# Two-layer vision tower with a graph-gated expert stage: how the edge keys reach their bins is changed

## The chip, the cores and the metric

The kernel runs on one core of a Trainium2 chip, as one program with one launch. Its time is the device time in microseconds (us); the engines are TensorE (PE, with its weight loads as PEld), VectorE (DVE), ScalarE (ACT), GpSimd (POOL) and SyncE (SP).

## The reference, cut to what matters

64 images of 84 x 84 become 64 tokens of 64 features each (4096 tokens, in 32 chunks of 128). Four parts follow, each added to its input and layer-normed: attention across images, 8 small experts with one softmax gate per token place, a linear recurrence over the tokens of an image, and 4 experts of which a graph network picks two per token. The change touches the preparation of that graph network's edges:

```python
src = jnp.concatenate([edge_index[0], loops])     # 262144 edges, indices drawn from 0 .. 16383
dst = jnp.concatenate([edge_index[1], loops])
e = leaky_relu(a_src[src] + a_dst[dst])
e_max = segment_max(e, dst); ee = exp(e - e_max[dst])
denom = segment_sum(ee, dst)
agg = segment_sum(h[src] * (ee / denom[dst])[:, :, None], dst)
```

Only 4096 nodes exist; a source beyond them is taken as the last node, a destination beyond them drops the edge. So the kernel counts, per destination, the edges whose source is that last node (`n_far`) and keeps as keys only the near ones, some 1 in 16 of all. These must be grouped by destination node. They are made from the input at run time.

## The kernel before, in words

Four expert and attention stages follow one another, each a `Block` in which every engine has its own program; all engines meet at the end of a block. Within it the order is the written one on each engine, and semaphores tie the engines together.

`tokens_and_counts` (0 to 204 us) makes the tokens and, from the edge list, one f32 key per near edge: `bin` (destination modulo 128), `loc` (destination divided by 128, 0 to 31) and source, plus one. The edges lie 2048 to a partition, wherever they came. `G.rounds` is the number of rounds of 16 keys that the fullest partition needs, `G.batches` the number of batches of 256.

`attention0_and_sort` (204 to 345 us) sorts each partition's keys on VectorE (`sort_batch`), builds for each of up to 256 positions `t` a one-hot row of the key's bin (`bin_one_hot`, 128 x 128 per position), and lets TensorE add these up, so that each key learns its rank within its bin over all partitions: the count of the bin in earlier partitions, read by `look_up` (L906), and its place in its own run. The slot of a key in DRAM is bin times 2^18 plus rank (`slot_index`), its value (`slot_key`) holds `loc` and source. Then the keys are exchanged: GpSimd issues one indirect DMA per position `t`, 128 keys of 4 bytes each, to `bin_slots` in DRAM (`scatter_round`, L536, 16 positions a round). The rounds are spread: round 0 in `attention0_and_sort`, which also waits for it, rounds 1 to 8 in `experts0`, rounds 9 to 15, as far as they exist, in `attention1`, whose GpSimd waits for all of them and then signals `all_slots_written`. The rest of `attention0_and_sort`, normalization and the turn of the tokens to features, runs on the other engines.

`experts0` (345 to 604 us) computes the 8 experts in 4 pairs for 4 groups of 1024 tokens: 16 steps `n`. A step is `layer1(n)` (two matmuls of 512 f32 columns, L1086), ScalarE's relu (L1158), `layer2(n)` (four matmuls, L1098), and VectorE's gated product (L1201), which reads PSUM and the gate rows. TensorE runs layer1 of a step and layer2 of the step before; layer2 waits for the gated products before. After each fourth step `out(g)` (32 f32 matmuls, each with two records in the trace as all f32 matmuls here, L1111) adds the experts up, and VectorE adds the tokens (`residual`, L1172). At the end stand `ln.vector`, `tf.tensor` and `tf.vector`, norm and turn. Two PSUM banks (6 and 7) take the outputs in turn.

`attention1` (604 to 785 us) needs the list early: SyncE loads 256 slots per bin (`load_list`, 128 KB) once `all_slots_written` is there, bins on partitions, and VectorE sorts them in 32 rounds of 8, 14 of which (`EARLY_SORT`) stand ahead of its first read of TensorE's step sums (L1483), the rest in later gaps. ScalarE's relus of the state (L1439) and TensorE's sums over it (L1352) go on beside this.

`graph_and_experts` (785 to 1268 us) gathers one node row per list place with 160 indirect DMAs (L1734), 16 places a group, as many groups as the fullest bin needs, beside the 4 experts, and then works on the list on VectorE; `combine` ends the kernel.

## Time and profile before

| | |
|---|---|
| time, median of 3 runs | 1319.32 us (1307.67 to 1325.57) |
| the profiled execution | 1305.82 us, its span 1304.0 us |
| mean granted TensorE clock | 0.619 |
| busy: PE, PEld, DVE, ACT, POOL | 493.0, 398.9, 639.1, 129.3, 361.3 us |
| `attention0_and_sort`, 204 to 345 us | DVE 100.6 us busy, POOL 17.6 |
| `experts0`, 345 to 604 us | PE 107.2 us busy, DVE 41.7, ACT 30.3, POOL 124.7 |
| `attention1`, 604 to 785 us | PE 133.3 us busy, DVE 110.7, POOL 21.6 |
| load of the list, 128 KB, issue to landing | 3.3 us |
| SBUF to DRAM scatters, SBUF from DRAM gathers | 160 and 160 indirect DMAs |

The busy times are of one execution. The span runs from its first instruction to its last; some 2 us lie around it. Each stage's busy times stand against its length: in `experts0` no engine is busy for half of its 259 us. The granted clock is TensorE's, as a share of 2.4 GHz; 0.50 is its lower level, 1.2 GHz.

### The profile page before, as it was taken

What the parts mean: (1) busy time and instruction counts of PE and PEld (TensorE: products, weight loads), DVE (VectorE), ACT (ScalarE), POOL (GpSimd) and SP (SyncE); (2) the same over time, 40 slices, a digit from 0 to 9 for tenths busy, and PEclk for the clock granted to TensorE, in tenths of its full rate; (3) what the DMA queues carried; (4) which work ended last, traced back from release to release, by engine and by line L of the source; (5) the groups of instructions that cost most, each with busy time, mean ns of one, the idle gap of its engine ahead of it and who ended that gap; (6) DMA issues with size and microseconds to landing.
All of it is one profiled execution on the core that took longest, in us unless ns stands there. A gap on an engine that the chain in (4) does not pass through costs nothing. (4 is left out here: it accounts for less than half of the span.)

```text
span 1304.0 us, 10802 instructions
## 1 busy us (share of the span) xinstructions
PE 493.0 (38%) x3438; PEld 398.9 (31%) x3438; DVE 639.1 (49%) x2388; ACT 129.3 (10%) x243; POOL 361.3 (28%) x373
## 2 busy tenths in 40 slices
PE   6945545380151122886699834101003830000000
PEld 6635443370120012554477832101002630000000
DVE  5999995795510000133576852000000159996067
ACT  2200000320110000132100012000010300000011
POOL 0000000000477773403300006777673000000712
PEclk9977778595555555685767656555555655555555
DMA  5000001000000000000000001111110000002101
GB/s 126 2 1 2 1 2 26 9 4 2 1 0 1 0 1 0 1 1 14 5 1 1 1 13 25 10 10 10 9 10 5 1 1 0 0 0 97 10 2 32
DMA packets 35618, 14.18 MB, mean 11 GB/s; under 512 B 30410, under 2 KB 35146, under 8 KB 35154
## 3 DMA queue, kind: packets, MB, share of 16 engines
q1 hardware_dynamic: 21376, 9.89, 2.9%
q0 software_dynamic: 11264, 2.46, 2.5%
q10 hardware_dynamic: 2904, 0.98, 0.5%
q8 instruction: 30, 0.49, 0.2%
q14 instruction: 44, 0.35, 0.1%
HBM read 8.51 MB, written 4.80 MB: 10 GB/s over the span
## 5 line engine op out<-in xcount | busy, mean ns | idle before, releaser
L536 POOL DMA_INDIRECT bin_slots<-slot_key,slot_index x160 | 158.0, 988 | 145.9 <-issue 145.9
L1734 POOL DMA_INDIRECT gathered<-node_table,list_src_i x160 | 152.2, 952 | 53.7 <-issue 53.7
L1780 DVE TENSOR_TENSOR expert_out<-bank,e_b 128x512 f32<-128x512 f32 x16 | 11.0, 691 | 241.0 <-issue 88.2
L1201 DVE SCALAR_TENSOR_TENSOR e_h2w<-bank,e_low,e_gate_rows 128x512 f32<-128x512 f32 x32 | 23.2, 748 | 181.3 <-remote 115.4
L427 PE MATMUL bank<-dst_one_hot 128*128 128x128 bf16 x1024 | 73.7, 247 | 67.8 <-DVE dst_one_hot L490 67.8
L427 PEld LDWEIGHTS bank<-dst_one_hot 128*128 128x128 bf16 x1024 | 72.4, 113 | 69.5 <-DVE dst_one_hot L490 69.5
L1740 POOL DMA_INDIRECT node_rows<-segment_table,segment_end_i x32 | 30.3, 946 | 220.0 <-DMA segment_table<-segment_rows 210.6
L1768 PE MATMUL bank<-e_w,segment_rows 128*128 128x64 f32 x256 | 47.5, 363 | 87.6 <-issue 43.3
L490 DVE TENSOR_SCALAR dst_one_hot<-dst_hi 128x256 bf16<-128x256 bf16 x512 | 75.9, 435 | 1.1 <-ACT edge_keys_then_tokens L372 1.1
L490 DVE TENSOR_SCALAR dst_one_hot<-dst_lo 128x256 bf16<-128x256 bf16 x512 | 75.1, 454 | 0.0
L1768 PEld LDWEIGHTS bank<-e_w,segment_rows 128*128 128x128 f32 x256 | 46.0, 278 | 92.9 <-issue 46.7
L1755 PE MATMUL bank<-h_features,e_w 64*128 64x512 f32 x64 | 28.5, 919 | 115.0 <-issue 89.5
L1111 PE MATMUL bank<-e_wo,e_h2w 128*128 128x64 f32 x256 | 49.6, 374 | 32.1 <-issue 30.6
L1098 PE MATMUL bank<-e_h,e_w 64*64 64x512 f32 x128 | 23.4, 812 | 98.5 <-DVE e_h2w L1201 65.5
L1111 PEld LDWEIGHTS bank<-e_wo,e_h2w 128*128 128x128 f32 x256 | 49.3, 292 | 35.8 <-issue 33.5
L1755 PEld LDWEIGHTS bank<-h_features,e_w 64*128 64x128 f32 x64 | 14.5, 290 | 124.9 <-issue 95.9
L392 POOL PARTITION_ALL_REDUCE left_max<-left_keys x1 | 0.4, 352 | 168.2 <-DVE left_keys L511 168.2
L1158 ACT ACTIVATE e_h<-bank,e_B,e_A 128x512 f32<-128x512 f32 x32 | 23.8, 775 | 205.8 <-PE bank L1086 137.3
L1589 POOL IOTA fill_slot_i<- 128x8 int32 x1 | 0.1, 133 | 151.0 <-issue 151.0
L1794 ACT ACTIVATE segment_rows<-bank,e_b 128x512 f32<-128x512 f32 x32 | 19.2, 702 | 219.6 <-issue 167.6
L1098 PEld LDWEIGHTS bank<-e_h,e_w 64*64 64x64 f32 x128 | 4.0, 161 | 115.1 <-DVE e_h2w L1201 75.9
L906 DVE CUSTOM_DVE_ANT_0 rank_prod<-bank,bin_one_hot 128x128 f32<-128x128 f32 x160 | 34.6, 286 | 0.6 <-DVE slot_key L898 0.3
(381 smaller groups left out, 1056.9 us busy)
## 6 DMA issues: line engine op xcount, KB each, us to landing
segment_table<-segment_rows SPq DMA_DIRECT2D x1, 3072.0 KB, 8.7
bin_slots<-slot_key,slot_index POOLq DMA_INDIRECT x160
gathered<-node_table,list_src_i POOLq DMA_INDIRECT x160
dst_one_hot<-in_L_ffn_edge_index SPq DMA_DIRECT2D x2, 1024.0 KB, 7.0
out_dram<-edge_keys_then_tokens SPq DMA_DIRECT2D x4, 256.0 KB, 3.6
images<-in_x SPq DMA_DIRECT2D x2, 441.0 KB
images<-in_x ACTq DMA_DIRECT2D x2, 441.0 KB
e_w<-in_L_ffn_W SPq DMA_DIRECT2D x6, 128.0 KB
```

Of the source, the lines that this page charges most:

```text
L427: ins = pe.matmul(G.bank[0][:, 0:P], hot[u][:, b, 0:64, i:i + PAIR], hot[u][:, b, 64:P, i:i + PAIR], start=False, stop=True, skip_group_ch ...
L490: ins = dve.tensor_scalar(hot[q % 2][:, :, at + v, :], x, float(v), None, ALU.is_equal)
L536: pool.indirect_dma_start(A["slots"], bass.IndirectOffsetOnAxis(ap=G.slot_idx[:, t:t + 1], axis=0), G.slot_key[:, t:t + 1], None, bounds_c ...
L906: o.mark(dve.tensor_tensor_reduce(out=prod[:, t, :], in0=G.bank[6][:, 0:P], in1=hot[:, c, :], scale=1.0, scalar=0.0, op0=ALU.mult, op1=ALU ...
L1098: ins = pe.matmul(G.bank[4 + u][rows_of(e ^ u), :], w.W2[rows_of(e), q, :], H1[rows_of(e), n % 2, u, :], start=True, stop=True, skip_group ...
L1111: ins = pe.matmul(G.bank[6 + g % 2][:, c * D:(c + 1) * D], H2w[:, g % 2, u, q, i * P:(i + 1) * P], w.Wo[:, u, q, :], start=(q == 0), stop= ...
L1158: act.activation(H1[:, n % 2, u, :], G.bank[2 * (n % 2) + u][:, :], ACT.Relu, bias=w.par["B1"][:, q:q + 1], scale=w.par["A1"][:, q:q + 1]) ...
L1201: dve.scalar_tensor_tensor(out=H2w[:, g % 2, u, q, :].rearrange("p (b f) -> p b f", f=T), in0=G.bank[4 + u][:, :].rearrange("p (b f) -> p ...
L1734: pool.indirect_dma_start(Gt[:, j, :], None, A["table"], bass.IndirectOffsetOnAxis(ap=G.src_i[:, j:j + 1], axis=0)).then_inc(gat, 16)
L1740: pool.indirect_dma_start(N[:, c, :], None, A["ends"], bass.IndirectOffsetOnAxis(ap=end_i[:, c:c + 1], axis=0)).then_inc(ends_in, 16)
L1755: pe.matmul(G.bank[2 * (n % 3) + u][:, :], W1[r, e, :], G.hT[r, g * TILE:(g + 1) * TILE], start=True, stop=True).then_inc(l1_mm, 1)
L1768: ins = pe.matmul(G.bank[6 + n % 2][:, (u * EXP1 + e) * D:(u * EXP1 + e + 1) * D], HH[:, u, e, h * P:(h + 1) * P], W2[:, e, :], start=True ...
```

## The change

The scatter through DRAM is kept as a fallback. In its place, where each partition has at most 160 keys (`ALWAYS`, 10 rounds) and each bin at most 192 (`SENT_RANKS`), the keys go from partition to partition through TensorE, in `experts0`. A key is cut into two numbers that bf16 holds exactly (`key_high`, `key_low`). For each of 160 positions `t` GpSimd makes two rows of 192 places in SBUF, the place with the key's rank holding the number and all others zero (`tensor_scalar`: equal to the rank, times the number). TensorE multiplies the position's bin one-hot (128 x 128) with these 384 columns and adds all 160 products up in one PSUM bank: row is bin, column is rank. GpSimd makes batches of 8 positions in four buffers; TensorE takes them up in `send(q)`: 0 and 1 in the head of the stage, `q = n + 2` in step `n`, and the last, 19, ahead of the last `out`. VectorE puts the two halves together after the turn. Bank 7 is thereby taken: the outputs share bank 6, the small matmuls of the head are laid out anew, and the bias row is copied to SBUF. `scatter_rounds` is computed at run time, 0 if the keys are sent; the loops of the scatter and its waits go by it. In `attention1` the list is still loaded from DRAM (into `list_by_scatter`), where the slots hold -1 if nothing was scattered, and VectorE takes the maximum of both. The sort's one-hots and ranks stay in SBUF through `experts0`, and the thresholds of nodes in the list are shifted by a constant bit.

```diff
@@ -46,6 +46,13 @@
 EARLY, MIDDLE = 1, 9
+SENT = 16 * ALWAYS
+SENT_RANKS = 192
+SEND = 8
+SEND_BUFS = 4
+KEY_BITS = 17
+KEY_SET = 1 << KEY_BITS
+KEY_LOW = 9
...
@@ -538,9 +545,15 @@
+def rounds_to_scatter(G, eng):
+
+    return (eng.value_load(G.scatter_rounds[0:1, 0:1], min_val=0, max_val=EW // 16),
+            eng.value_load(G.batches[0:1, 0:1], min_val=1, max_val=EW // SORTED))
+
+
 def scatter_last_batch(G, A, pool, scat, rounds):
-    m, n = batch_rounds(G, pool)
+    m, n = rounds_to_scatter(G, pool)
     for j in rounds:
...
@@ -640,6 +657,7 @@
                 pool.partition_all_reduce(tmx[:, :], tmax[:, :], P, bass.bass_isa.ReduceOp.max).then_inc(cmax_s, 1)
+                pool.wait_ge(asked_s, 1)
                 scatter_last_batch(G, A, pool, scat_last, range(0, EARLY))
...
@@ -883,16 +901,20 @@
                                              ALU.logical_shift_left))
-                    o.mark(dve.tensor_scalar(loc_i[:, :], k_i[:, :], 12, NC - 1, ALU.arith_shift_right,
-                                             ALU.bitwise_and))
+                    o.mark(dve.tensor_scalar(hi_i[:, :], k_i[:, :], KEY_SET - 1, KEY_LOW, ALU.bitwise_and,
+                                             ALU.logical_shift_right))
+                    o.mark(dve.tensor_scalar(lo_i[:, :], k_i[:, :], (1 << KEY_LOW) - 1, None, ALU.bitwise_and))
                     o.mark(dve.tensor_tensor(cont[:, 1:SORTED], bin_f[:, 1:SORTED], bin_f[:, 0:SORTED - 1],
                                              ALU.is_equal))
-                    o.then(dve.tensor_scalar(k_i[:, :], k_i[:, :], NTOK - 1, None, ALU.bitwise_and))
-                    o.mark(dve.tensor_scalar(loc_i[:, :], loc_i[:, :], 13, None, ALU.logical_shift_left))
+                    o.then(dve.tensor_scalar(k_i[:, :], k_i[:, :], KEY_SET - 1, KEY_SET, ALU.bitwise_and,
+                                             ALU.bitwise_or))
+                    o.mark(dve.tensor_copy(G.key_high[:, :], hi_i[:, :]))
+                    o.mark(dve.tensor_copy(G.key_low[:, :], lo_i[:, :]))
                     o.mark(dve.tensor_scalar(pad_i[:, :], pad_i[:, :], BIN_BITS + 8, None, ALU.logical_shift_left))
                     o.then(dve.tensor_tensor_scan(pos[:, :], cont[:, :], cont[:, :], 0.0, ALU.mult, ALU.add))
-                    o.mark(dve.tensor_tensor(k_i[:, :], k_i[:, :], loc_i[:, :], ALU.bitwise_or))
+                    o.mark(dve.tensor_scalar(G.key_high[:, :], G.key_high[:, :], 1.0, None, ALU.add))
+                    o.mark(dve.tensor_scalar(G.key_low[:, :], G.key_low[:, :], -float(1 << KEY_LOW - 1), None, ALU.add))
                     o.then(dve.tensor_tensor(bin_i[:, :], bin_i[:, :], pad_i[:, :], ALU.bitwise_or))
...
@@ -932,7 +954,10 @@
+                f.mark(dve.tensor_copy(r_f[:, :], G.rounds[:, :]))
                 f.then(dve.tensor_scalar(tmax[:, :], tmx[:, :], float(PART), 1.0, ALU.min, ALU.max))
+                f.mark(dve.tensor_scalar(over[:, 0:1], r_f[:, :], float(ALWAYS), None, ALU.is_gt))
+                f.mark(dve.tensor_scalar(over[:, 1:2], tmx[:, :], float(SENT_RANKS), None, ALU.is_gt))
                 f.then(dve.tensor_scalar(tmax[:, :], tmax[:, :], 15.0, None, ALU.add))
...
@@ -941,6 +966,11 @@
                 f.then(dve.tensor_copy(G.passes[:, :], p_i[:, :]))
+
+                f.then(dve.tensor_tensor(over[:, 0:1], over[:, 0:1], over[:, 1:2], ALU.max))
+                f.then(dve.tensor_tensor(r_f[:, :], r_f[:, :], over[:, 0:1], ALU.mult))
+                f.then(dve.tensor_copy(G.scatter_rounds[:, :], r_f[:, :]))
+                dve.sem_inc(asked_s, 1)
...
@@ -1067,11 +1097,26 @@
         N = NG * NPAIR
-        a2_rows, logits, bias = G.bank[7][:, 0:NPAIR * D], G.bank[6][:, 0:EXP0], G.bank[6][:, 256:256 + D]
-        gates_t, bo_b2, gate_rows = G.bank[5][0:EXP0, 0:P], G.bank[5][0:EXP0, P:P + D], G.bank[7][:, :]
+        place = st.sb("place_one_hot_times_key", [P, SEND_BUFS, SEND, 2, SENT_RANKS], BF16)
+        bias_kept = st.sb("e0_bias", [P, D])
+        sent_low = st.sb("sent_low", [P, SENT_RANKS])
+        a2_rows, logits, bias = G.bank[5][:, 0:NPAIR * D], G.bank[4][:, 0:EXP0], G.bank[5][:, 256:256 + D]
+        gates_t, bo_b2, gate_rows = G.bank[4][0:EXP0, P:2 * P], G.bank[6][0:EXP0, 0:D], G.bank[6][:, :]
+        sent = G.bank[7][:, 0:2 * SENT_RANKS]
         with nc.Block() as block:
             @block.gpsimd
             def _(pool):
+                for q in range(SENT // SEND):
+                    if q >= SEND_BUFS:
+                        pool.wait_ge(sent_s, q - SEND_BUFS + 1)
+                    for i in range(SEND):
+                        t = q * SEND + i
+                        for k, key in enumerate((G.key_high, G.key_low)):
+                            ins = pool.tensor_scalar(place[:, q % SEND_BUFS, i, k, :], G.iota[:, :], G.rank[:, t:t + 1],
+                                                     key[:, t:t + 1], ALU.is_equal, ALU.mult)
+                    ins.then_inc(made_s, 1)
                 scatter_last_batch(G, A, pool, G.middle_written, range(EARLY, MIDDLE))
...
@@ -1099,16 +1144,24 @@
+                def send(q):
+
+                    pe.wait_ge(made_s, q + 1)
+                    for i in range(SEND):
+                        t = q * SEND + i
+                        ins = pe.matmul(sent, G.hot[:, t, :],
+                                        place[:, q % SEND_BUFS, i, :, :].rearrange("p k r -> p (k r)"),
+                                        start=(t == 0), stop=(t == SENT - 1), skip_group_check=True)
+                    ins.then_inc(sent_s, 1)
+
                 def out(g):
                     pe.wait_ge(gw_s, 2 * NPAIR * (g + 1))
-                    if g == 0:
-                        pe.wait_ge(tm_s, NG)
-                    if g >= 2:
-                        pe.wait_ge(o_s, g - 1)
+                    if g >= 1:
+                        pe.wait_ge(o_s, g)
                     for c in range(GC):
                         i, u = c // 2, c % 2
                         for q in range(NPAIR):
-                            ins = pe.matmul(G.bank[6 + g % 2][:, c * D:(c + 1) * D], H2w[:, g % 2, u, q, i * P:(i + 1) * P],
+                            ins = pe.matmul(G.bank[6][:, c * D:(c + 1) * D], H2w[:, g % 2, u, q, i * P:(i + 1) * P],
                                             w.Wo[:, u, q, :], start=(q == 0), stop=(q == NPAIR - 1))
...
@@ -1125,6 +1178,7 @@
                 layer1(1)
+                send(0)
                 pe.wait_ge(gate_s, 1)
...
@@ -1136,13 +1190,17 @@
                 pe.matmul(bias, gT[:, :], bo2[:, :], start=True, stop=True).then_inc(bias_mm, 1)
+                send(1)
+                pe.wait_ge(kept_s, 1)
                 for n in range(N + 1):
                     if 2 <= n < N:
                         layer1(n)
                     if n >= 1:
                         layer2(n - 1)
+                    send(n + 2)
                     if n >= 5 and n % NPAIR == 1:
                         out(n // NPAIR - 1)
+                send(N + 3)
                 out(NG - 1)
...
@@ -1194,6 +1252,9 @@
                 o.then(dve.tensor_copy(wrep[:, :, :, :].rearrange("p u q f -> p (u q f)"), gate_rows))
+                dve.wait_ge(bias_mm, 1)
+                dve.tensor_copy(bias_kept[:, :], bias).then_inc(kept_s, 1)
+                dve.wait_ge(kept_s, 1)
...
@@ -1222,6 +1283,13 @@
                 tf.vector(dve, G)
+                dve.wait_ge(sent_s, SENT // SEND)
+                o.mark(dve.memset(G.raw[:, SENT_RANKS:PART], -1.0))
+                o.then(dve.tensor_copy(sent_low[:, :], sent[:, SENT_RANKS:2 * SENT_RANKS]))
+                o.then(dve.scalar_tensor_tensor(out=G.raw[:, 0:SENT_RANKS], in0=sent[:, 0:SENT_RANKS],
+                                                scalar=float(1 << KEY_LOW), in1=sent_low[:, :], op0=ALU.mult, op1=ALU.add))
+                o.then(dve.tensor_scalar(G.raw[:, 0:SENT_RANKS], G.raw[:, 0:SENT_RANKS],
+                                         float(KEY_SET - (1 << KEY_LOW - 1)), None, ALU.add))
...
@@ -1466,6 +1535,7 @@
                 dve.wait_ge(list_in, 16)
+                o.then(dve.tensor_tensor(G.raw[:, :], G.raw[:, :], scattered[:, :], ALU.max))
                 sort_list(G, dve, o, range(0, EARLY_SORT))
```

## Rows read from the trace of the kernel before

**Rows 1.** Stretches: length, each engine's busy us (instructions), granted clock, DMA share, GB/s.

```profile
372.00:523.20 151.20, 29.68 (x112) 17.59 (x110) 9.88 (x14) 6.22 (x8) 99.74 (x103) 0.51 0.02 1
...
570.50:604.00 33.50, 23.05 (x114) 18.23 (x113) 12.85 (x24) 7.86 (x12) 0.00 (x0) 0.63 0.00 1
```

**Rows 2.** Instructions in time, TensorE: start, us, engine, line, operation, tiles, [idle before].

```profile
409.35 1.98 PE L1098 MATMUL bank<-e_h,e_w 64*64 64x512 f32 x8 [25.44 <-DVE e_h2w L1201]
...
523.22 2.08 PE L1086 MATMUL bank<-h_features,e_w 64*128 64x512 f32 x4
...
527.14 1.48 PE L1086 MATMUL bank<-h_features,e_w 64*128 64x512 f32 x4
...
557.09 1.09 PE L1098 MATMUL bank<-e_h,e_w 64*64 64x512 f32 x8 [0.45 <-DVE e_h2w L1201]
...
559.67 1.09 PE L1098 MATMUL bank<-e_h,e_w 64*64 64x512 f32 x8 [0.44 <-DVE e_h2w L1201]
```

**Rows 3.** Instructions in time, an output matmul beside the scatters.

```profile
502.33 0.27 PE L1111 MATMUL bank<-e_wo,e_h2w 128*128 128x64 f32 x1 [2.54 <-issue]
```

**Rows 4.** Stretches of ones-matmuls and of output matmuls of groups 2 and 3.

```profile
268.80:277.70 8.90, 8.90 (x161) 8.90 (x161) 7.87 (x52) 0.00 (x0) 0.00 (x0) 1.00 0.01 5
...
563.30:570.60 7.30, 7.30 (x70) 7.23 (x66) 1.41 (x2) 0.00 (x1) 0.00 (x0) 1.00 0.01 2
...
579.40:593.30 13.90, 13.90 (x64) 13.72 (x64) 0.00 (x0) 0.00 (x0) 0.00 (x0) 0.50 0.00 1
```

**Rows 5.** The page's costliest groups, and GpSimd in time at two starts.

```profile
L536 POOL DMA_INDIRECT bin_slots<-slot_key,slot_index x160 | 158.0, 988 | 145.9 <-issue 145.9
...
358.65 0.97 POOL L536 DMA_INDIRECT bin_slots<-slot_key,slot_index  x1 [14.13 <-issue]
...
523.21 0.97 POOL L536 DMA_INDIRECT bin_slots<-slot_key,slot_index  x1 [20.37 <-issue]
```

**Rows 6.** Instructions in time, the start of the stage `attention1`.

```profile
608.86 6.07 PE L1363 MATMUL bank<-h_features,dx_t 64*128 64x512 f32 x16 [6.96 <-DMA decay<-in_c_decay]
...
628.93 2.06 ACT L1439 ACTIVATE state_x<-bank 128x512 f32<-128x512 f32 x4 [12.98 <-remote]
...
632.26 0.43 DVE L1242 MAX8 list_sorted<-list_raw 128x8 f32<-128x256 f32 x1 [14.41 <-DMA list_raw<-bin_slots]
...
634.16 1.99 PE L1363 MATMUL bank<-h_features,dx_t 64*128 64x512 f32 x8
...
636.07 7.17 PE L1352 MATMUL bank<-state_x,pick_chunk 128*32 128x128 f32 x64
...
646.39 0.28 DVE L1483 COPY step_sums<-bank 32x128 f32<-32x128 f32 x1
```

**Rows 7.** The page's costliest groups, the gathers of the last expert stage.

```profile
L1734 POOL DMA_INDIRECT gathered<-node_table,list_src_i x160 | 152.2, 952 | 53.7 <-issue 53.7
```

**Rows 8.** Groups of GpSimd by form, and its first two sums in time.

```profile
L1590 POOL IOTA fill_bin<- 128x8 int32 x1 | 0.1, 125 | 0.0
...
L1322 POOL MEMSET gathered<- 128x6144 f32 x1 | 5.2, 5218 | 2.4 <-issue 2.4
...
1268.61 1.06 POOL L2011 TENSOR_TENSOR mix_tmp<-expert_out,gates 128x512 f32<-128x512 f32 x1 [24.91 <-POOLq L1698]
...
1269.75 1.59 POOL L2012 TENSOR_TENSOR mix<-mix_tmp,edge_keys_then_tokens 128x512 f32<-128x512 f32 x1
```

**Rows 9.** Instructions in time, VectorE's last in the first expert stage.

```profile
602.99 0.18 DVE L1229 COPY mean_square_of_tokens<-mean_square_of_ln 128x32 f32<-128x32 f32 x1
```

**Rows 10.** Groups by form, then single waits, in time order of the prediction.

```profile
L896 DVE TENSOR_TENSOR bin_i<-bin_i,pad_i 128x256 int32<-128x256 int32 x1 | 0.4, 417 | 0.0
...
L898 DVE CAST slot_key<-key_i 128x256 f32<-128x256 int32 x1 | 0.3, 294 | 0.0
...
356.62 3.61 DVE L1180 TENSOR_REDUCE e_feat<-h_features 128x64 f32<-128x2048 f32 x1 [11.54 <-PEq L173]
...
629.06 5.22 POOL L1322 MEMSET gathered<- 128x6144 f32 x1 [2.38 <-issue]
```

55 lines of the change are left out of this document (34 added, 21 removed).

## The prediction, made before the changed kernel was run

> **What bounds the kernel now.** I read the stretches first, then single instructions where the change touches. One stretch is out of proportion [rows 1]: from 372.00 to 523.20 us, in the first expert stage, TensorE is busy 29.68 us of 151.20, VectorE 9.88, ScalarE 6.22, and GpSimd 99.74. The last 33.5 us of the stage, with GpSimd idle, hold nearly as much TensorE work, 23.05 us. So the stage is not bound by work. One step of it shows how: a second layer at 409.35, beside the scatters, comes after a wait of 25.44 us; without them the one at 559.67 comes 2.58 us after the one at 557.09, with a wait of 0.44 [rows 2]. Even the output matmuls, which wait for nothing between each other, stand 2.5 us apart beside the scatters [rows 3], and the 64 records of one group take 7.30 us or 13.90 without, at a granted clock of 1.00 or 0.50 [rows 4]. The scatters are 160 indirect DMAs of 0.988 us: 16 before the stage, 128 in it, 16 after it [rows 5]. What the others wait for in that time is signals and issue, not data. After GpSimd had paused for 20.37 us, they ran at their normal pace for some steps although it scattered again [rows 2, 5]. I read it as a backlog which the indirect DMAs build up in whatever carries completions; the trace shows when it is there, not its mechanism.
>
> The second place is the start of the next stage: VectorE waits 14.41 us for the list, which SyncE may load only once all scatters have landed, and ScalarE waits 12.98 us in the same time [rows 6]. The chain that ended last lies in the final stage, which the change leaves alone; but every stage ends with all engines meeting, so what a stage gains or loses, the total does.
>
> **The change, part by part.** *The scatters go*, if at run time there are at most 10 rounds and at most 192 keys in the fullest bin. 160 scatters are 10 rounds of 16; 160 gathers are 10 groups of 16, so the fullest bin has at most 160 keys [rows 5, 7]. Both hold. That the change would not do what it says is thereby out.
>
> *GpSimd makes places*: 320 instructions of 128 x 192, bf16 in and out, a comparison with one number per partition and a product with another. No row shows this form. The nearest [rows 8]: an iota of 8 elements takes 125 ns, a memset of 6144 5218 ns, so 125 ns and 0.83 an element, which gives 0.29 us. A two-input tensor_tensor of 512 elements takes 1.06 us the first time, (1060 - 125)/512 = 1.83 ns an element, which gives 0.48 us; beside a busy VectorE 1.59, 2.86 ns an element, 0.67 us. One tensor input, two numbers per partition and two operations lie between the first two, nearer the second, as reading the numbers must cost something: I take 0.42 us, the gap to the next included. 320 x 0.42 = 134 us from 358.65, where the stage's first GpSimd instruction starts now [rows 5], to 493.1. The GPSIMD Engine Reference of the Trainium skill (3.1) has a loop with 1.8 cycles an element, 769 ns for 512; by that an instruction would be some 0.41 us, an estimate, and the sum the same within 4 us.
>
> *TensorE sends*: 160 matmuls of 384 bf16 columns. Some 160 ones-matmuls of 128 columns took 8.90 us, 0.056 each, at a granted clock of 1.00, 2.4 GHz [rows 4]. Three times that is 0.17 us, at 1.2 GHz 0.34: 27 or 54 us. They stand in program order behind waits for GpSimd, so layers 1 and 2 queue behind a send that is late. TensorE's own pace: at full clock a step of 2.58 plus 8 x 0.17, less the 0.44 of idle that a send fills, 3.5 us; 16 steps 56 us, three outputs of 7.30, 22 us; from 372 to 450. At half clock a step is 3.92 (523.22 to 527.14) plus 2.7 less 0.8, 5.8; 93 + 3 x 13.90 = 135 us, to 507 [rows 2, 4]. GpSimd's 493 is later than the first, and with GpSimd as the pace TensorE is still busy most of the time; I take GpSimd's.
>
> *After the last place*: a send of 1.3 us; the last output, 7.30 or 13.90, 10.6 taken; from the last output's end at 593.30 to 603.17 the residual, norm and turn, 9.8 us [rows 4, 9]; and four operations of 128 x 256 or less for the list's keys, 0.27 to 0.43 us each, 1.3 [rows 10]. Together 23.0 us: the stage ends at 516.1 instead of 603.2, a gain of 87.1 us.
>
> *Small edits.* VectorE's bias copy lies beside the wait for the first gated rows. Its four token adds get two SBUF inputs; were each held up for as long as a two-input operation of GpSimd's, 1.59 us, that is 6 us under waits for TensorE, and GpSimd's pace decides: nothing. One output bank instead of two: the residual that frees it is one operation, done a group ahead. Nothing.
>
> *The sorting stage*: three more operations of 0.29 us or less and six on single elements, at most 2.6 us on VectorE [rows 10]. GpSimd's wait for its 16 writes to land goes. Its last scatter ended at 344.52, 14.13 before 358.65, and such a wait was 2.38 us in the later stage; so until about 346.9, against VectorE's end at 345.08 [rows 5, 10]: -1.8. I take 0; bounds -8 and +1 on the time, as the 11.54 us until VectorE's next instruction may hold more of the landing than I see.
>
> *The next stage*: the list's load is issued right after the weights, of which those that TensorE needs have landed at 608.86, and takes 3.3 us, so it lands before VectorE asks at 617.85. The 14.41 us go, a maximum of 128 x 256 (0.42) comes; VectorE would read TensorE's step sums at 632.4, not at 646.39. Late next are these sums. They ended at 643.2, after ScalarE's 12.98 us and irregular issue on TensorE, both in the scatters' time. Without these, in program order, 6.07 us from 608.86, then 3.6, 1.99, 3.6, 1.99 and 7.17: 633.3 [rows 6]. So 13.1 of the 14.0 us come. Were TensorE's clock at half from 618.5 on, they would end near 648, and the gain be nothing.
>
> **The sum**: 87.1 + 13.1 = 100.2 us off the profiled execution's 1305.8: 1205.6. That execution is 1.0% under the median shown, 1319.3, and near the fastest shown, 1307.7; the new median may stand from even with the sum to 1% above, and I put it at 1210.
>
> **The rivals.** *TensorE's pace* (chance 0.15). If a place costs 0.29 us, GpSimd ends at 451 and TensorE decides: at full clock the stage ends at 450 + 19.7, a gain of 133.5 and 13.1 more, 1159; at half clock at 507 + 27.6, 68.6 and 13.1, 1224. For it: the rates of memset and iota. Against: these read no tensor.
>
> *GpSimd becomes a longer bound than the scatters* (0.07). Its place: the 320 instructions ahead of the last send. 100 us are gained at 0.42 us each, so 0.73 is even, and from 0.81 on the kernel is over 2% (26 us) slower. The only longer GpSimd rows for so few elements are the indirect DMAs', 0.97 us; at 0.98 the places end at 672, the stage at 695, and the kernel takes 1305.8 + 92 - 13 = 1385. For it: no comparison on GpSimd has a row. Against: that is twice the two-input price. The same page (3.1) gives 12 cycles an element for data-dependent branching; if the comparison branched, an instruction would be near 1.9 us, an estimate, and the kernel beyond 1650; no row here shows such a loop.
>
> *In between* (0.08): 0.65 to 0.81 us a place, as beside a busy VectorE [rows 8]; 1280 to 1331, no difference. Against: VectorE is busy only 9.88 of 151.20 us here, and its gated products read PSUM and one SBUF tensor.
>
> *The stall stays* (0.04). If it comes from GpSimd's being busy and not from its DMAs, the 151 us remain, only the list's wait goes, and up to 54 us of sends come: 1293 to 1347. For it: the trace shows only that the two coincide. Against: the steps after 523 were normal while GpSimd worked.
>
> The rest, 0.66, is the forecast: GpSimd's pace at 0.30 to 0.64 us a place.
>
> **How the numbers follow.** A measurement of this kernel tells some 2% from no change. Faster by more: 0.66 + 0.15 = 0.81. Within 2%: 0.08, and 0.02 of the stall, 0.10. Slower: 0.07, and 0.02 of the stall, 0.09. Range: low is TensorE's full-clock bound, 1159, less some us for the sorting stage's bound, 1155. High is a place at 0.64 us, 1206 + 320 x 0.22 = 1276, so 1275. In between, the slower rival and the stall are left out, 0.19.
>
> **What would show it.** No indirect DMA before the gathers. GpSimd's instructions 0.42 us apart from the stage's start, TensorE's second layers about 7 us apart, with sends that wait for GpSimd. The first expert stage 171 us long, not 258. No wait for the list in the next stage, and 13 us less of it. It is wrong if a place costs over 0.65 us, or if signals come late beside GpSimd's arithmetic too. The gathers of the last expert stage stay as they are; should that stage change its length, something is at work that I don't see.

## The result, and the profile after

The kernel after takes **1384.53 us** (median of 4 runs, 1378.89 to 1390.74), the kernel before beside it 1319.11 us: ratio **1.0507**, 95% interval 1.0419 to 1.0595. It is slower by 5%; 1210 us was forecast. The profiled execution has a span of 1380.3 us for 1304.0. The numbers of one rival, a GpSimd instruction of 0.98 us and a kernel of 1385 us, are near what came.

The page's costliest groups of the kernel after, against the scatters and the waits of [rows 5]. Columns: line, engine, operation, tiles, shapes, count, busy us, mean ns, idle time before them and what ended it.

```profile
L1117 POOL TENSOR_SCALAR place_one_hot_times_key<-ranks_iota,rank_f,key_high 128x192 bf16<-128x192 bf16 x160 | 160.7, 1004 | 32.3 <-issue 32.3
L1117 POOL TENSOR_SCALAR place_one_hot_times_key<-ranks_iota,rank_f,key_low 128x192 bf16<-128x192 bf16 x160 | 161.1, 1007 | 0.0
L1262 DVE SCALAR_TENSOR_TENSOR e_h2w<-bank,e_low,e_gate_rows 128x512 f32<-128x512 f32 x32 | 22.6, 747 | 240.8 <-PE bank L1143 240.8
L1152 PE MATMUL bank<-place_one_hot_times_key,bin_one_hot 128*128 128x384 bf16 x160 | 51.2, 496 | 194.5 <-POOL place_one_hot_times_key L1117 194.5
```

An instruction takes 1.00 us, not 0.42. TensorE stands 194.5 us in front of places that are not there yet, and VectorE 240.8 us in front of TensorE. GpSimd in time, first and last instruction of its row:

```profile
355.39 1.03 POOL L1117 TENSOR_SCALAR place_one_hot_times_key<-ranks_iota,rank_f,key_high 128x192 bf16<-128x192 bf16 x1 [32.29 <-issue]
...
671.61 1.01 POOL L1117 TENSOR_SCALAR place_one_hot_times_key<-ranks_iota,rank_f,key_low 128x192 bf16<-128x192 bf16 x1
```

From start to start that is (671.61 - 355.39)/319 = 0.991 us, without a gap. The stretches of the kernel after, with the columns of [rows 1]: the whole first expert stage, then the part beside the places and the part behind them.

```profile
347.80:700.50 352.70, 149.83 (x673) 84.06 (x673) 42.12 (x69) 29.70 (x43) 317.22 (x320) 0.62 0.00 0
...
372.00:673.00 301.00, 122.14 (x548) 61.97 (x547) 28.15 (x42) 21.82 (x31) 300.62 (x304) 0.64 0.00 0
673.00:700.50 27.50, 19.64 (x88) 18.03 (x86) 8.86 (x19) 3.41 (x5) 0.00 (x0) 0.55 0.00 1
```

GpSimd is busy 300.62 of 301.00 us, TensorE 122.14: GpSimd is what bounds the stage. The ledger of the two profiled executions follows. The borders are VectorE's first instruction in the first expert stage, its first in the next stage, its read of the step sums, GpSimd's iota at the head of the last expert stage, and the end.

| stretch | before | after | difference |
|---|---|---|---|
| start of the first expert stage at | 356.62 | 347.75 | -8.9 |
| first expert stage | 247.1 | 352.8 | +105.7 |
| next stage, to the step sums | 42.6 | 29.9 | -12.7 |
| from there to the last expert stage | 138.9 | 122.1 | -16.8 |
| from there to the end | 518.8 | 527.7 | +8.9 |
| span | 1304.0 | 1380.3 | +76.3 (rounded parts: +76.2) |

### The profile page after: what moved, and what is told of

It reads as the page before. It is cut to its first block and busy times, and to the rows that moved or that the text cites. A ratio compares the mean times of both kernels' runs of the same rounds, so it can differ in the third digit from the quotient of the medians.

```text
span 1380.3 us, 11128 instructions
## 1 busy us (share of the span) xinstructions
PE 525.7 (38%) x3598; PEld 408.7 (30%) x3598; DVE 640.6 (46%) x2403; ACT 129.3 (9%) x243; POOL 520.9 (38%) x533
## 5 line engine op out<-in xcount | busy, mean ns | idle before, releaser
L1117 POOL TENSOR_SCALAR place_one_hot_times_key<-ranks_iota,rank_f,key_high 128x192 bf16<-128x192 bf16 x160 | 160.7, 1004 | 32.3 <-issue 32.3
L1117 POOL TENSOR_SCALAR place_one_hot_times_key<-ranks_iota,rank_f,key_low 128x192 bf16<-128x192 bf16 x160 | 161.1, 1007 | 0.0
L1262 DVE SCALAR_TENSOR_TENSOR e_h2w<-bank,e_low,e_gate_rows 128x512 f32<-128x512 f32 x32 | 22.6, 747 | 240.8 <-PE bank L1143 240.8
L1850 DVE TENSOR_TENSOR expert_out<-bank,e_b 128x512 f32<-128x512 f32 x16 | 11.1, 692 | 247.7 <-remote 131.5
L1152 PE MATMUL bank<-place_one_hot_times_key,bin_one_hot 128*128 128x384 bf16 x160 | 51.2, 496 | 194.5 <-POOL place_one_hot_times_key L1117 194.5
L434 PEld LDWEIGHTS bank<-dst_one_hot 128*128 128x128 bf16 x1024 | 74.6, 116 | 66.8 <-DVE dst_one_hot L497 66.8
L1152 PEld LDWEIGHTS bank<-place_one_hot_times_key,bin_one_hot 128*128 128x128 bf16 x160 | 19.7, 134 | 232.9 <-POOL place_one_hot_times_key L1117 199.6
L1825 PEld LDWEIGHTS bank<-h_features,e_w 64*128 64x128 f32 x64 | 15.3, 304 | 119.6 <-ACT segment_rows L1864 96.0
L1164 PEld LDWEIGHTS bank<-e_wo,e_h2w 128*128 128x128 f32 x256 | 43.5, 268 | 0.7 <-issue 0.7
L1164 PE MATMUL bank<-e_wo,e_h2w 128*128 128x64 f32 x256 | 42.9, 352 | 0.0
```

The lines of the kernel that those rows point to most:

```text
L434: ins = pe.matmul(G.bank[0][:, 0:P], hot[u][:, b, 0:64, i:i + PAIR], hot[u][:, b, 64:P, i:i + PAIR], start=False, stop=True, skip_group_ch ...
L1117: ins = pool.tensor_scalar(place[:, q % SEND_BUFS, i, k, :], G.iota[:, :], G.rank[:, t:t + 1], key[:, t:t + 1], ALU.is_equal, ALU.mult)
L1152: ins = pe.matmul(sent, G.hot[:, t, :], place[:, q % SEND_BUFS, i, :, :].rearrange("p k r -> p (k r)"), start=(t == 0), stop=(t == SENT - ...
L1164: ins = pe.matmul(G.bank[6][:, c * D:(c + 1) * D], H2w[:, g % 2, u, q, i * P:(i + 1) * P], w.Wo[:, u, q, :], start=(q == 0), stop=(q == NP ...
L1262: dve.scalar_tensor_tensor(out=H2w[:, g % 2, u, q, :].rearrange("p (b f) -> p b f", f=T), in0=G.bank[4 + u][:, :].rearrange("p (b f) -> p ...
L1825: pe.matmul(G.bank[2 * (n % 3) + u][:, :], W1[r, e, :], G.hT[r, g * TILE:(g + 1) * TILE], start=True, stop=True).then_inc(l1_mm, 1)
```

## The experiments

Five batches of runs gave a surprise that belongs ahead of them. The kernel before, unchanged, took some 1075 us in four of these batches (medians 1075.65, 1073.52, 1078.55 and 1079.07) and 1314.76 us in one, as in the batch of the result. All its runs within a batch agree, and 1314.76 and 1078.55 came from the same chip. I call them the **long** and the **short condition**. So each kernel is set against the kernel before of its own batch, and stages are compared between profiles of one condition.

**1. Both kernels in the short condition.** No edit.

> The kernel before, unchanged, profiled beside the experiments. In the first batch its time was 1075.65 us (7 runs) for 1319.11 us beside the kernel after, and without the scatters 989.88 us: they cost 86 us there. Theory, the gap of 244 us lies in the two stretches in which GpSimd issues indirect DMAs: the first expert stage falls from 247 us to 170 to 190 us (160 scatters x 0.99 us = 158 us bound it, with nothing standing behind them), and the gather stage from 274 us to some 110 us, with everything up to the first expert stage within 5 us of what it was (356.6 us). Rival, all is faster in proportion (a higher clock everywhere): the first expert stage starts 15% earlier too, at 300 us.

> The kernel after, unchanged, beside the experiments. It made 1384.53 us beside a before of 1319.11 us. Theory P, the 1.00 us of GpSimd's instruction is its own wherever it runs: 320 of them hold 318 us, 318 - 237 = 81 us over the compare-alone kernel's 1144 us, so some 1225 us, 1.14 of the kernel before as it runs here (1075). Rival Q, the price too belongs to the condition that slowed the kernel before: the instruction takes some 0.76 us here, with or without the multiplication, and the kernel some 1145 us, 1.06 of the kernel before.

Measured: before 1072.83 us (one run; 7 runs of it beside the experiments 1073.52), after 1228.37 us, ratio **1.1403** (1.1328 to 1.1478). Theory P holds: GpSimd's instruction costs the same in both conditions. The theory on the kernel before holds too: of the 233.1 us between its two profiles (spans 1304.0 and 1070.9) 74.8 lie in the first expert stage and 149.5 behind the head of the last one (164 were expected), and the first expert stage starts only 2.5 us earlier.

```profile
L1117 POOL TENSOR_SCALAR place_one_hot_times_key<-ranks_iota,rank_f,key_high 128x192 bf16<-128x192 bf16 x160 | 161.1, 1007 | 31.6 <-issue 31.6
L1117 POOL TENSOR_SCALAR place_one_hot_times_key<-ranks_iota,rank_f,key_low 128x192 bf16<-128x192 bf16 x160 | 161.1, 1007 | 0.0
...
L1850 DVE TENSOR_TENSOR expert_out<-bank,e_b 128x512 f32<-128x512 f32 x16 | 11.1, 692 | 50.2 <-PE bank L1838 50.2
```

The stage after is 352.6 us here and 352.8 in the long condition: it has no indirect DMA, and no condition. The last line is in the last expert stage, where the gathers remain: VectorE idles 50.2 us, while in the result's profile of the same kernel it was 247.7. The kernel before, in the short condition: two stretches, then steps of TensorE to hold against [rows 2], then VectorE's first instruction in the next stage.

```profile
354.10:447.00 92.90, 79.43 (x498) 49.06 (x498) 37.06 (x57) 28.57 (x41) 69.25 (x72) 0.83 0.03 2
452.00:526.30 74.30, 0.00 (x0) 0.00 (x0) 0.00 (x0) 0.00 (x0) 51.82 (x54) 0.50 0.02 1
```

```profile
407.76 1.09 PE L1098 MATMUL bank<-e_h,e_w 64*64 64x512 f32 x8 [0.44 <-DVE e_h2w L1201]
408.78 1.13 PE L1086 MATMUL bank<-h_features,e_w 64*128 64x512 f32 x4
410.35 1.09 PE L1098 MATMUL bank<-e_h,e_w 64*64 64x512 f32 x8 [0.44 <-DVE e_h2w L1201]
```

```profile
526.34 0.11 DVE L1452 MEMSET pick_chunk<- 128x63 f32 x1 [74.42 <-PEq L1072]
```

This is another picture of the same code. Beside the scatters TensorE now makes a second layer every 2.59 us, with 0.44 us of wait. All compute is done by 452, and then everybody waits 74.42 us for GpSimd. Its row itself differs too. Here is the one pause in it and its last scatter of the stage, in the short condition and then, the scatter alone, in the long one (the pause there is the 20.37 us of [rows 5]):

```profile
505.34 0.97 POOL L536 DMA_INDIRECT bin_slots<-slot_key,slot_index  x1 [4.54 <-issue]
...
523.23 0.97 POOL L536 DMA_INDIRECT bin_slots<-slot_key,slot_index  x1 [0.30 <-issue]
```

```profile
541.11 0.97 POOL L536 DMA_INDIRECT bin_slots<-slot_key,slot_index  x1 [0.30 <-issue]
```

The pause stands ahead of the last 15 of the 128 scatters both times, and the kernel has no wait there; what it is, no run shows. The stage is 172.3 us for 247.1. Of the 74.8 us between, 15.3 are GpSimd's longer row (356.11 to 524.20 for 358.65 to 542.08), and 59.5 what stands behind it: 2.1 us here, 61.7 us of compute in the long condition, since the others' hand-overs crawl beside the row.

So in the short condition GpSimd's row is the bound before and after, 128 instructions every 1.28 us against 320 every 0.99. From 568.7 to 731.2, the step sums come 162.5 us later. In the long condition the change takes the crawl and the longer row away with the scatters. That is why it loses 76 us there and 158 here: 74.6 of the 81 us between the two losses lie in this stage (+105.7 and +180.3).

**2. What the scatters are worth.** All of them out; half of them (the waits for landings count half as many); a wait after each round.

```
def scatter_last_batch(...):  and  def wait_for_scatter(...):
+    return
```

> The kernel before, with the 160 scatters through DRAM left out and nothing in their place (the keys are not exchanged, so the lists are empty of meaning). Theory, the scatters cause the 151 us stretch in which the other engines stand with little to do: the first expert stage falls from 247 us to 100 to 130 us (TensorE's 107 us of busy time in it, less what runs beside), the landing wait before it (some 9 us) and the list wait behind it (some 13 us) go too, and the kernel comes to 1150 to 1190 us. Rival, the stall has another cause (a semaphore of the stage itself): the stage stays over 200 us and the kernel over 1260 us.

```
-    for t in range(16 * j, 16 * j + 16):
+    for t in range(16 * j, 16 * j + 8):
```

> The kernel before with 8 of the 16 scatters of each round left out, so that half the keys are not exchanged. All of them left out gave 86 us on a chip where the kernel before took 1075. Theory for such a chip, the stage ends with GpSimd's row of scatters and the others stand before it: 80 x 1.05 us = 80 us shorter, then held by TensorE as without any: within 10 us of 0.925 of the kernel before. Theory for a chip where it takes some 1315 us, the other engines' hand-overs crawl only while GpSimd issues: with half of the row the crawl ends 80 us sooner and the sums of the steps start at 560 to 575 us for 646, the kernel 70 to 90 us shorter. Rival for either, the cost is of each landing or of a fixed wait, not of the issue row: under 40 us gained.

```
             scatter_round(G, A, pool, j, scat)
+            pool.wait_ge(scat, 256 * (j - rounds[0] + 1))
```

> The kernel before, whole, with GpSimd waiting for the landing of its scatters after every round of 16. Theory, the scatters cost by GpSimd's issue time (158 us) and nothing piles up: each of the 10 waits adds a landing of about 2.5 us, 10 x 2.5 = 25 us at most: 1075 to 1100 us. Rival, a backlog of outstanding scatters slows the other engines: with at most 16 outstanding the kernel comes out faster than before, to 1030 to 1060 us.

All three fell in the short condition. Without scatters: 989.88 us, ratio 0.9204 (0.9158 to 0.925), stage 100.6 us. With half: 993.76 us, 0.9174 (0.9118 to 0.923), stage 103.0 us. The first expectation was worked out for the long condition, which no run without scatters met. Between the profiled spans of the kernel before and of the one without scatters, 1070.9 and 980.5 us, lie 90.4 us: 71.7 in the stage, 8.3 ahead of it, where the first 16 scatters land, 13.0 in the next, where the list is waited for, and the rest is 2.6 us longer without them. So the cost is in the main the row's overhang, as expected for half the scatters: half a row hides behind compute, and the second half makes the cost (993.76 us for 997.7, which is 0.925 of the kernel before). The wait after each round: 1113.53 us, 1.0317 (1.0239 to 1.0396), above the 25 us expected for the waits and against the backlog rival. GpSimd's idle time before its scatters is 97.1 us for 68.4: the landing waits are 23.5 of it, in 6 records, and the stage ends 29.6 us later (555.9 for 526.3). Another 7.4 us lie in the next stage, with the last two waits, and 6.3 in the recurrence part (below).

**3. What GpSimd's instruction is made of.** Half the columns, eight columns, no product.

```
+pool.memset(place[:, :, :, :, :], 0.0)
-pool.tensor_scalar(place[..., k, :], G.iota[:, :], G.rank[...], key[...], ALU.is_equal, ALU.mult)
+pool.tensor_scalar(place[..., k, 0:96], G.iota[:, 0:96], G.rank[...], key[...], ALU.is_equal, ALU.mult)
(or 0:8; or, at full width and without the memset: G.rank[...], None, ALU.is_equal)
```

> The kernel after, with GpSimd writing only the columns of ranks 0 to 95 of each place (128x96 in the place of 128x192); the buffers are blanked once before. It leaves out the keys of rank 96 and above. Theory A, the 0.99 us of an instruction is a price per instruction (fetching the two per-partition numbers, starting): the instruction stays at 0.9 us or more, the 320 of them take over 290 us, and the kernel stays at 1350 us or more. Theory B, it is a price per element, (1005 - 125) / 192 = 4.6 ns each with the 8-element iota of the kernel before as the start: 0.125 + 96 x 0.0046 = 0.57 us, 320 of them 182 us, and the first expert stage is about 135 us shorter: some 1245 us.

> The kernel after, with GpSimd writing only 8 of the 192 columns of each place; it leaves out the keys of rank 8 and above. By 1.005 us at 192 columns and 0.700 at 96, an element costs 3.2 ns and an instruction 0.39 us before its first: theory, linear: 0.39 + 8 x 0.0032 = 0.42 us. Rival, there is a floor or a step, so that the price is not a line: 0.6 us or more.

> The kernel after, with the multiplication by the key taken out of GpSimd's instruction: one comparison with one per-partition number, at the same 128x192. It leaves out the values of the keys (ones are sent). If each of the two operations costs a pass over the elements (theory B1), the instruction falls to about 0.5 to 0.6 us, the 320 of them to 160 to 190 us, and the kernel comes to about 1245 us. If the price is of the elements, whatever is done to them (B2), or of the instruction (A), it stays at 0.9 to 1.0 us and the kernel at 1350 to 1390 us.

The instructions of these kernels by tile, duration min/median/max in ns, start of the first and the last. Eight columns:

```profile
L1120 POOL TENSOR_SCALAR place_one_hot_times_key<-ranks_iota,rank_f,key_high x160: 385/478/937, 364.1 to 485.8; 128x8 bf16<-128x8 bf16 x160
L1120 POOL TENSOR_SCALAR place_one_hot_times_key<-ranks_iota,rank_f,key_low x160: 384/474/908, 364.5 to 486.1; 128x8 bf16<-128x8 bf16 x160
```

Half the columns:

```profile
L1120 POOL TENSOR_SCALAR place_one_hot_times_key<-ranks_iota,rank_f,key_high x160: 677/696/901, 364.5 to 578.8; 128x96 bf16<-128x96 bf16 x160
L1120 POOL TENSOR_SCALAR place_one_hot_times_key<-ranks_iota,rank_f,key_low x160: 677/696/1212, 365.2 to 579.5; 128x96 bf16<-128x96 bf16 x160
```

The comparison alone, 192 columns:

```profile
L1117 POOL TENSOR_SCALAR place_one_hot_times_key<-ranks_iota,rank_f x320: 750/757/1317, 355.2 to 591.6; 128x192 bf16<-128x192 bf16 x160
```

From start to start: (486.1 - 364.1)/319 = 0.382 us, (579.5 - 364.5)/319 = 0.674, and 0.991 for the whole place. The steps are 0.292 us for 88 columns and 0.317 for 96, 3.3 ns a column both times: **0.356 us and 3.3 ns a column**. Neither theory A nor B was right: a third is the instruction's, two thirds are the elements'. The fixed part I had expected for eight columns, 0.39, came from mean durations, which overlap their neighbours; starts are the better clock. The comparison alone is (591.6 - 355.2)/319 = 0.741 us, so the product and its second number cost 0.25 us of 0.99. That is neither a whole pass (B1) nor nothing (B2). The kernels took 1144.01, 1045.71 and 1144.45 us (one run each) beside a kernel before of 1075.65 (half width and comparison alone) and 1078.55 us. With eight columns the kernel is 3% under the kernel before even in the short condition, one run against 7. All these places are bf16 on 128 partitions; what another type would cost was not measured.

The Trainium skill, GPSIMD Engine Reference, section 3.1, gives 769 ns for 512 elements of a tight loop, 1.5 ns each; the same line of mine would be 2.05 us for 512, an estimate from the rows above. The measurement decides: that page's loop is not this instruction.

**4. The sends alone.** The places are blanked once, TensorE sends zeros.

```
-                    for i in range(SEND):
-                        ... pool.tensor_scalar(...) ...
+                        ... pool.memset(place[:, q % SEND_BUFS, :, k, :], 0.0)      # first four batches
+                    if q >= SEND_BUFS:                                               # the other 16
+                        pool.memset(place[:, q % SEND_BUFS, 0, 0, 0:2], 0.0).then_inc(made_s, 1)
```

> The kernel after, with GpSimd's 320 comparisons left out: the places are blanked once and TensorE sends zeros, in the same 160 matmuls of 384 columns and the same 20 hand-overs. It leaves out the keys. Theory, TensorE then paces the stage: the kernel without scatters and without sends took 990 us; 160 sends at 0.21 to 0.32 us of new time each (361 ns busy in the kernel with VectorE's places) add 35 to 50 us, so 1020 to 1040 us. Rival, the sends fit in TensorE's pauses: 1000 us or less. It bounds what any maker of places can reach with this exchange.

1001.50 us, ratio 0.9309 (0.9247 to 0.937); stage 112.6 us, 12.0 over the one without any exchange. That is 1.5 us over the rival's 1000 and under the 1020 to 1040 expected: the sends nearly fit in TensorE's pauses. TensorE's part of the change was never a problem. The rival *TensorE's pace* had the stage end near 470 us at full clock (450 and 19.7); it ends at 461.0, with a granted clock of 0.89 from 350 to 400 us and of 1.00 from 400 to 450.

**5. The places on VectorE, whole.** The same instruction on another engine, in batches between VectorE's gated products.

```
 for n in range(N):
     for u in range(2):
         gated(n, u)
+    make(n + 4)          # make(0) to make(3) ahead of the loop
 def make(q):  dve.wait_ge(sent_s, ...);  16 x dve.tensor_scalar(place..., G.iota..., G.rank..., key..., is_equal, mult)
```

> The kernel after, whole, with the 320 places made by VectorE between its own steps of the stage, in the place of GpSimd. Theory, GpSimd's 0.99 us an instruction is the whole of the loss: VectorE's two-scalar comparison takes some 0.13 to 0.15 us for this size, 320 of them 42 to 48 us beside its own 43 us of the stage; the stage then goes by TensorE, whose busy time in it was 8.5 + 122.1 + 19.6 = 150 us in the kernel after. Stage 140 to 180 us for 352.8 us, kernel 1170 to 1210 us, about 0.90 of the kernel before. Rival, the sends themselves (160 matmuls in 20 batches, each waiting for a hand-over) hold the stage over 220 us: kernel over 1247 us.

1043.41 us, ratio **0.9669** (0.9619 to 0.972) in the short condition: faster than both kernels. The expected time was worked out from the long condition's levels and does not apply; the stage does.

```profile
L1234 DVE TENSOR_SCALAR place_one_hot_times_key<-ranks_iota,rank_f,key_high x160: 308/326/336, 355.4 to 478.6; 128x192 bf16<-128x192 bf16 x160
```

```profile
348.00:501.00 153.00, 109.42 (x669) 63.22 (x665) 117.19 (x389) 29.77 (x43) 0.00 (x0) 0.88 0.00 1
```

The stage is 153.5 us, within the 140 to 180 expected. An instruction here takes VectorE (117.19 - 42.12)/320 = 0.235 us of busy time (42.12 is its own work, from the stretch of the kernel after), not the 0.13 to 0.15 expected from the constant comparison; still a quarter of GpSimd's 0.991. Only the engine that makes the places changed, and the stage goes from 352.6 to 153.5 us, under the 172.3 of the kernel before: the loss was what a place costs on GpSimd.

**6. Sharing the places.** Three ways: VectorE compares once and multiplies twice; ScalarE makes the low products; GpSimd makes every fourth batch. This batch fell in the long condition.

```
+ same = (iota == rank)               # VectorE, once a column
+ place_high = same * key_high        # VectorE
+ place_low  = same * key_low         # VectorE (compare once) or ScalarE (scalar low)
```

```
 def make(q):                         # VectorE
+    if q % 4 == 3: return            # these 5 batches: GpSimd, fused, with a semaphore of their own
```

> The kernel with VectorE's places, whole, where VectorE compares once for each column of 128 edges and multiplies that by the high and by the low part of the key in two further instructions, each with one operation and one per-partition number. The fused instruction took 0.326 us (52 us for 160), while a comparison of 256 elements by a constant took 0.147 us in the stage before (75 us for 512). Theory, VectorE's price lies in the second operation: three instructions at 0.11 to 0.15 us are 0.33 to 0.45 us a column for 0.65: 53 to 72 us for 104, and the kernel comes from 1043 to 1000 to 1030 us. Rival, it lies in the per-partition number: each still takes 0.25 to 0.33 us, 120 to 156 us in all, and the kernel stays or rises: 1045 to 1090 us.

> As the kernel with one comparison a column, whole, but the multiplication by the low part done by ScalarE (160 instructions of 192 elements, some 0.3 us each by the 0.775 us of its 512-element ReLU: 50 us beside its own 38 us of the stage). Theory, VectorE is then under TensorE's pace: the kernel comes within 15 us of the sends alone, 1001 us: 1000 to 1020 us. Rival, the extra hand-over through ScalarE holds up its ReLUs, which TensorE waits for: 1030 to 1060 us.

> The kernel with VectorE's fused places, whole, but every fourth batch of 16 places made by GpSimd: 5 batches x 16 x 1.0 us = 80 us on GpSimd, 15 x 16 x 0.326 = 78 us on VectorE for 104. Theory, the engines work side by side and VectorE's 104 us was what held the stage over the sends alone (1043 for 1001 us): 26 us less on VectorE give 1015 to 1030 us. Rival, the two engines slow each other while both run (GpSimd's instruction goes over 1.2 us or VectorE's over 0.4 us): 1040 us or more.

The kernel before took 1314.76 us here. Compare once: 1194.64 us, 0.9076 (0.9044 to 0.9108). ScalarE: 1239.60 us, 0.9399 (0.9356 to 0.9443). Split: 1177.39 us, **0.8941** (0.8898 to 0.8985). So in the condition of the result, the exchange by TensorE with the places shared makes this kernel 11% faster. Neither side of compare once came true: its three instructions a column take 3 x (128.88 - 42.12)/480 = 0.54 us of VectorE (128.88 is its busy time in that stage), over the two fused ones' 0.47. The times expected for all three were for the short condition; only the split was run there too (below). The stage of the split kernel and GpSimd's places in it:

```profile
347.30:496.80 149.50, 114.44 (x673) 64.66 (x673) 104.33 (x310) 29.87 (x43) 83.54 (x80) 0.82 0.00 1
```

```profile
L1118 POOL TENSOR_SCALAR place_one_hot_times_key<-ranks_iota,rank_f,key_high x40: 1000/1076/1284, 354.2 to 465.7; 128x192 bf16<-128x192 bf16 x40
```

With ScalarE the stage is 198.4 us, the longest of the three variants' stages. The sends wait 58.8 us for its products, but no matmul of the stage waits for a relu; so ScalarE does hold the stage up, as its rival had it, but through the places and not through the relus. Its 160 products took (85.34 - 29.70)/160 = 0.35 us each.

```profile
L1147 PE MATMUL bank<-place_one_hot_times_key,bin_one_hot 128*128 128x384 bf16 x160 | 41.0, 416 | 58.8 <-ACT place_one_hot_times_key L1218 58.8
```

Then the split kernel again and its variant with the comparison once, on one chip, in the short condition:

```
 split kernel, and in make(q): one is_equal and two mult per column, as above
```

> The split kernel again, for the comparison on one chip with its variant, and as a test of the theory that the chips differ only where GpSimd issues indirect DMAs. It has none in the first expert stage. Theory: where the kernel before takes some 1075 us, this one keeps the start of its steps' sums at 520 to 532 us (525.9 before) and saves 190 us in the gather stage alone: 985 to 1025 us. Rival, the other chip is quicker in all stages: the sums start under 510 us.

> The split kernel, whole (every fourth batch of places by GpSimd), with VectorE's three quarters made by one comparison and two multiplications a column. Those took 0.190 us an instruction (30.3 us for 160), the fused one 0.326: 0.57 for 0.65 us a column, so 120 x 0.08 = 10 us less on VectorE. Theory, VectorE still holds the stage: 5 to 10 us under the split kernel beside it. Rival, TensorE's 150 us of work and its hand-overs hold it by now: within 3 us of the split kernel. Against the kernel before: 0.89 where that takes some 1315 us, 0.94 to 0.96 where it takes some 1075.

The split: 1025.50 us, **0.9492** (0.9424 to 0.956), step sums at 529.0 for 525.9 in the long condition. The stage without scatters doesn't know the condition, as expected: 151.7 us here, 149.4 there, while VectorE's wait in the last expert stage is 50.2 and 244.0. Behind the last expert stage's head 155 us went, not the 190 expected, so the time lies at the edge of its range. With the comparison once: 1035.99 us, 0.9589 (0.9547 to 0.963), which neither side had expected; VectorE's busy time in the stage is 114.11 us for 104.30.

```profile
348.70:507.60 158.90, 117.45 (x673) 65.52 (x673) 114.11 (x430) 29.80 (x43) 82.08 (x80) 0.81 0.00 1
```

That expectation and the one of compare once priced the fused instruction at 0.326 us, its duration; but neighbours overlap (0.31 us instructions start 0.24 us apart), and it costs 0.235. In the short condition's split kernels, beside a working GpSimd, the two fused instructions of a column cost 2 x (104.30 - 42.12)/240 = 0.52 us, the three single ones (114.11 - 42.12)/120 = 0.60. And the split's own expectation, 26 us off VectorE: its stage is 151.7 us for 153.5, and the kernel's other 16 us lie behind the stage, where nothing was edited. Here is the recurrence part, first the kernel with VectorE's places, then the split one:

```profile
530.30:675.30 145.00, 109.85 (x512) 96.65 (x512) 93.84 (x233) 9.94 (x18) 0.02 (x1) 0.59 0.02 3
```

```profile
529.00:656.60 127.60, 100.47 (x512) 87.43 (x512) 93.80 (x233) 9.93 (x18) 0.00 (x0) 0.65 0.00 1
```

The work is the same 512 matmuls; the granted clock (the column before the last two) is 0.59 and 0.65. The two are from different batches, so how much of the difference belongs to the edit stays open. In the stage itself VectorE's pace is not what holds it any more: it gives up 12.9 us and the stage gives 2.

**7. The condition.** Three runs more, for the case that the long condition should come.

> The kernel before without its 160 scatters, once more, for the case that the kernel before takes some 1315 us beside it (it has taken 1315 and 1079 us on one chip, in two batches). Theory for that case, the scatters' issue is what makes the hand-overs of the first expert stage crawl: the sums of the steps start at 470 to 480 us, as where the kernel before takes 1075 us, for 646 with the scatters; the gather stage stays at some 275 us, as it keeps its own indirect DMAs; in all 1315 - 170 = some 1145 us. Rival, the crawl belongs to the stage and not to the scatters: the sums start after 550 us. Where the kernel before takes some 1075 us: 990 us, as before.

> The kernel before with 8 of 16 scatters a round (half the keys are not exchanged), for the same case. Theory, the crawl lasts as long as GpSimd issues: 80 x 1.05 = 84 us for 168, after which the stage goes on at its own speed: the sums start at 555 to 575 us for 646, the kernel at some 1235 us. Rival, a crawl that outlasts the issue (a backlog that is worked off later): sums after 600 us. Where the kernel before takes some 1075 us: 994 us, as before.

> The kernel before, whole, with a wait for the landing after each 16 scatters, for the same case. Theory, the hand-overs crawl through the issue itself: each wait gives the other engines only its own 2.5 to 5 us, and the kernel comes out at the kernel before plus 0 to 40 us. Rival, they crawl through the number of scatters under way: with at most 16 of them the stage takes under 200 us for 247 and the kernel under 1290 us. Where the kernel before takes some 1075 us: 1114 us, as before.

It did not: the kernel before took 1079.07 us, these 982.61, 989.80 and 1117.06, as in the first round. They confirm the short condition and say nothing of the long one.

## Why the prediction was wrong

**The step that failed is *GpSimd makes places*, 0.42 us an instruction.** Measured: 0.991. I had bounds from an iota, a memset and a two-input operation [rows 8] and took them for the form at hand, though none has a comparison, a number per partition, or two operations. The line that the runs give, 0.356 us and 3.3 ns a column, has three times the fixed part and four times the slope of the memset's. The dearest arithmetic row, 0.67 us, was one of another form too. The only thing that spoke for more was put aside as "no comparison on GpSimd has a row": true, and a reason for a wide bound, not for a chance of 0.07. An operation without a row, issued 320 times in a row on the engine that sets the pace, multiplies its error by 320: 0.57 us too little is 183 us. That the longer rival had 0.98 us is luck: it was the duration of an indirect DMA's issue, another kind of instruction, and not worked out from anything that a place does.

**The sum with the measured price is near.** With 0.991 us it gives places until 675.8, a stage until 698.8 and 1388 us for the profiled execution, which took 1382.05. Places went from 355.39 to 672.6 (671.61 and an instruction); then 27.9 us to the next stage's first instruction for the 23.0 of *After the last place*. The rival at 0.98 us had the kernel at 1385; that it meets the 1384.53 so closely owes something to chance, since 4.9 us more behind the last place and 7.9 us less behind the change (below) partly cancel.

**The stall** went, as foreseen: beside GpSimd's arithmetic TensorE and VectorE wait for places and for each other, and the 256 records of output matmuls in the kernel after, L1164, have no idle time before them, where the one of [rows 3] stood 2.54 us behind the last. But the stall was not a property of the kernel alone: in the short condition there is none, and what the scatters cost there, 86 us (1075.65 to 989.88), is in the main their row's overhang. In the long condition no run took the scatters out alone; the split kernel gains 137 us there (1314.76 to 1177.39) and 53 in the short one. I had read the stall as "a backlog in whatever carries completions", and the waits after each round, which keep the number under way small, were no help in the short condition; in the long one that wasn't tried. What causes the long condition, and by which way it delays signals only while GpSimd issues indirect DMAs, stays open.

**The next stage**: -12.7 us measured for -13.1. **The sorting stage**: I took 0 with a bound of -8, and -8.9 came; in the short condition it was -4.6 (354.1 to 349.5). The landing of the first 16 scatters was in that gap: VectorE's idle time ahead of the stage is 9.57 us in the short condition, and 1.57 where only the scatters are left out; in the result's profiles it is 11.54 and 1.58. **TensorE sends**: 160 sends take 51.2 us of busy time in the kernel after, within the 27 to 54; hidden in GpSimd's time, as said. By themselves they lengthen the stage by only 12.0 us.

**Behind the change** 16.8 us went and 8.9 came that no step had. The 16.8 are the recurrence part, 138.80 us in the kernel before:

```profile
646.40:785.20 138.80, 103.31 (x512) 89.54 (x512) 93.92 (x233) 9.94 (x18) 0.00 (x0) 0.63 0.02 3
```

and in the kernel after:

```profile
730.50:852.60 122.10, 93.18 (x512) 81.82 (x512) 93.59 (x233) 9.93 (x18) 0.00 (x0) 0.70 0.00 1
```

The same 512 matmuls again, at a granted clock of 0.63 and 0.70. In all twenty profiles, in both conditions, this part took between 122.1 and 145.2 us: a spread of 23 us that no edit here aims at, and as large as the 2% that decide. In the short condition the difference was -5.3. The 8.9 us are in the stages with the gathers, where the hand-overs crawl in the long condition; in the short one these stages differ by 0.4 us.

## What to carry to other kernels

An instruction that a change issues hundreds of times on one engine must have a row of its own form, or a measurement, before anything is summed; without one, the range has to reach past the dearest row of that engine (here the indirect DMAs' 0.97 us, which was close only by chance), and the chance of that end is not small. Price a row of instructions by its starts, since durations overlap: a fused instruction of 0.33 us cost 0.235. And before paying for the removal of a stall, look whether the stall is the kernel's or the condition's: beside the same scatters the other engines crawled in one batch and kept their pace in the next.

## What the runs showed of the hardware that I had not expected

- GpSimd's two-number comparison and product: 0.356 us and 3.3 ns for each of its columns, on 128 partitions; 0.25 us of the 0.99 for the product. VectorE does it in 0.235 us, ScalarE a product alone in 0.35.
- Beside one another, in the split kernel, both grew a little: GpSimd's median went from 1004 to 1076 ns, VectorE's low products from 325 to 349 ns.
- A memset on GpSimd held up VectorE. In the kernel with half the columns:

```profile
347.01 10.34 POOL L1112 MEMSET place_one_hot_times_key<- 128x12288 bf16 x1 [24.60 <-POOLq L180]
```

```profile
350.71 6.68 DVE L1242 TENSOR_SCALAR e_feat<-e_feat 128x64 f32<-128x64 f32 x1
```

  The 64-element operation, 0.20 us in the kernel after, ends at 357.39, just behind the memset's end at 357.35; with eight columns, and the same memset, it took 6.67 us. The Trainium skill, GPSIMD Engine Reference, section 1, says that GpSimd shares SBUF interfaces with VectorE, with contention for VectorE's instructions in a 2-port perf mode or with two SBUF inputs. This trace shows such a contention for an instruction with one tensor input, as a wait until the memset's end; whether that instruction ran in a 2-port mode, no row shows. Beside GpSimd's places, in the kernel after, no VectorE instruction waited like this.
- The same kernel took 1314.76 and 1078.55 us on one chip in two batches, each steady within itself, with the difference in the stages in which GpSimd issues indirect DMAs: in profiles of the kernel before, VectorE's wait in the last expert stage is 241.0 us in the long condition and 47.9 in the short one.
